# A two-layer graph network on one core: one-hots of the first column chunk by gather, remainders of five x tiles on GpSimd, one transpose moved

## The reference, cut to what matters

```python
agg = segment_sum(x[src], dst, num_segments=1250)
h   = (1 + eps) * x + agg
h   = relu(batch_norm(h @ W1 + b1, g1, be1))      # 512 -> 1024
h   = relu(batch_norm(h @ W2 + b2, g2, be2))      # 1024 -> 512
x   = layernorm(x + (x + h))
h   = relu(x @ V1 + c1) @ V2 + c2                 # 512 -> 256 -> 512
x   = layernorm(x + h + segment_sum(h[dst], src, num_segments=1250))
```

## Time and profile before

| | |
|---|---|
| median of 3 runs | 249.57 us (249.5 to 250.74) |
| the profiled execution | 249.95 us, of which the span takes 248.1 us |
| mean granted clock of TensorE | 0.995 of full speed |
| PE busy | 231.0 us, 93% of the span |
| DVE busy | 156.2 us, 63% |
| ACT busy | 134.2 us, 54% |
| POOL busy | 88.0 us, 35% |
| chain that ended last, by engine | PE 70%, DVE 12%, DMA 7%, ACT 6% |

### The profile page before, as it was taken

How to read it: one execution, slowest core, us unless ns; L and a number is a source line. 1 busy time by engine, 2 the same in 40 slices (tenths; PEclk the granted TensorE clock), 3 DMA queues, 4 the chain that set the end, 5 groups by cost and what they waited for, 6 DMA issues and landing times.

```text
span 248.1 us, 3897 instructions
## 1 busy us (share of the span) xinstructions
PE 231.0 (93%) x1454; PEld 197.3 (80%) x1454; DVE 156.2 (63%) x362; ACT 134.2 (54%) x233; POOL 88.0 (35%) x83
## 2 busy tenths in 40 slices
PE   0858999999999999999999999999999999999990
PEld 0845997777888888888888888888889997888970
DVE  1669899873966344555544316264876899796374
ACT  0656774763868067444455504457471639936373
POOL 5420000004920006565554500423456459701251
PEclk9999999999999999999999999999999999999998
DMA  3467800000066501111000087503209920000334
GB/s 100 156 214 214 202 0 3 1 3 3 3 261 239 198 1 45 42 42 45 0 0 0 4 206 142 106 3 60 45 4 170 202 85 3 0 0 0 131 127 160
DMA packets 32323, 19.96 MB, mean 80 GB/s; under 512 B 21927, under 2 KB 27084, under 8 KB 32302
## 3 DMA queue, kind: packets, MB, share of 16 engines
q1 hardware_dynamic: 31796, 19.45, 28.6%
q0 software_dynamic: 160, 0.13, 0.2%
q10 hardware_dynamic: 346, 0.10, 0.2%
HBM read 8.51 MB, written 5.92 MB: 58 GB/s over the span
## 4 chain that ended last, share of the span: by engine, by line
PE 70%; DVE 12%; DMA 7%; ACT 6%; issue 2%; POOL 1%; SPq 1%; DVEq 0%
PE ps L1281 22%; PE ps L1220 17%; PE ps L1298 11%; PE ps L1344 9%; PE ps L1362 6%; PE ps L1311 3%; DVE hot_s L849 3%; DMA plane_T<-planes 2%; PE ps L1200 2%; DMA src_i<-in_src 2%; DVE xT L984 2%; DMA pairs<-pair 2%; ACT planes L715 1%; DVE small_t L942 1%; DMA run<-pairs,start_i 1%
## 5 line engine op out<-in xcount | busy, mean ns | idle before, releaser
L942 DVE BATCH_NORM_STATS2 small_t<-ps 128x6 f32<-128x500 f32 (+1 forms) x36 | 21.6, 599 | 38.7 <-PE ps L1281 25.2
L1220 PE MATMUL ps<-AT,xh 128*128 128x500 f32 (+2 forms) x120 | 42.6, 366 | 0.4 <-ACT AT L569 0.4
L1220 PE MATMUL ps<-AT,xl 128*128 128x500 f32 (+2 forms) x120 | 40.9, 352 | 0.0
L1281 PE MATMUL ps<-h0h,wh 128*128 128x500 f32 (+1 forms) x96 | 33.9, 353 | 0.0
L1281 PE MATMUL ps<-h0h,wl 128*128 128x500 f32 (+1 forms) x96 | 33.9, 353 | 0.0
L1281 PE MATMUL ps<-h0l,wh 128*128 128x500 f32 (+1 forms) x96 | 33.8, 352 | 0.0
L485 POOL TENSOR_TENSOR wl<-w2s,wh 128x512 fp32r<-128x512 f32 x8 | 11.1, 1384 | 43.9 <-ACT wh L689 43.9
L480 POOL TENSOR_TENSOR wl<-w1s,wh 128x512 fp32r<-128x512 f32 x8 | 10.1, 1301 | 45.7 <-ACT AT L569 45.7
L1220 PEld LDWEIGHTS ps<-AT,xh 128*128 128x128 f32 (+1 forms) x120 | 22.6, 188 | 3.3 <-ACT AT L569 0.6
L1220 PEld LDWEIGHTS ps<-AT,xl 128*128 128x128 f32 (+1 forms) x120 | 22.7, 189 | 2.7
L1298 PE MATMUL ps<-a1h,wh 128*128 128x500 f32 (+1 forms) x96 | 23.7, 355 | 0.0
(11 more groups left out here) (148 smaller groups left out, 508.2 us busy)
## 6 DMA issues: line engine op xcount, KB each, us to landing
turns<-half_out SPq DMA_DIRECT2D x10, 320.0 KB, 2.2
out<-x SPq DMA_DIRECT2D x9, 256.0 KB
w1s<-in_L_gnn_W SPq DMA_DIRECT2D x4, 512.0 KB, 7.1
w2s<-in_L_gnn_W SPq DMA_DIRECT2D x8, 256.0 KB, 2.7
xs<-in_x SPq DMA_DIRECT2D x1, 1280.0 KB, 7.9
xs<-in_x SPq DMA_DIRECT2D x1, 1024.0 KB
lws<-in_L_gnn_W SPq DMA_DIRECT2D x1, 512.0 KB, 4.0
lw2s<-in_L_gnn_W SPq DMA_DIRECT2D x1, 512.0 KB, 4.2
```

Source lines behind the costliest of these rows:

```text
L942: link(nc.vector.bn_stats(stats[:, 6 * c:6 * c + 6], ps[:, zbank(t, c), 0:c1 - c0]))
L1220: last = mm(o, part[0:r, k, d * P:d * P + P], AT[0:r, k, c0:c1], start=(k == 0 and j == 0), stop=(k == NT - 1 and j == 1))
L1281: last = mm(ps[:, zbank(t, c), 0:c1 - c0], w[:, t, d * P:d * P + P], h[c][:, d, :], start=(d == 0 and j == 0), stop=(d == DT - 1 and j == 2))
```

## The change

**Keys.** The tiles `keyT` and `loT` keep their size, but their first 50 columns are used in another order: first the 25 windows of chunk 0 for c = 0, then the same windows for c = 1 (`keyW`, `loW`). `early_keys(c)` splits these 25 columns of one gather; `late_keys(c)` splits the other 100 windows later, behind the one-hots of group 4. The 50 columns make up groups 0 to 4 in this order, so groups 0 and 1 need the first gather alone, group 2 needs both, groups 3 and 4 the second. ACT copies them out with another pattern, in two pieces for group 2 (`early_out`). PSUM banks 6 and 7 hold the transposed runs until `late_keys` has read them; fill-in matmuls go to bank 4. The DVE queue waits for `keys_read` before it reads the flag.

**Remainders.** `xl` of tiles 5 to 9 is made by POOL, each when its `xh` is there, and `low_at` is gone.

**Transposes.** x's tile 5 is transposed once behind `build(3)`, tile 6 behind `build(5)` in the fast branch (PE has by then added tile 0's sums), where it was transposed behind `build(4)` before. Tiles 7 and 8 go one and two groups later.

```diff
         def x_bank(k):
-            return 3 + k if k < half else 6 + k % 2
+            return 3 + k if k < half else 5 if k == half else 6 + k % 2
+
+        key_bank, fill_bank = (6, 7), 4
...
-        cols_at = {6: half + 2, 7: half + 3, 11: half + 4}
-        turn_at = {6: half + 2, 7: half + 3, 12: half + 4}
+        cols_at = {5: half + 1, 7: half + 2, 9: half + 3, 11: half + 4}
+        turn_at = {5: half + 1, 7: half + 2, 9: half + 3, 12: half + 4}
         high_at = {5: half, 8: half + 1, 9: half + 2, 10: half + 3, 11: half + 4}
-        low_at = {7: half, 10: half + 1, 11: half + 2, 12: half + 3, 13: half + 4}
-        early_cols = {EARLY - 3: half, EARLY - 1: half + 1}
+        early_cols = {EARLY - 2: half}
...
+            for j, k in enumerate(range(half, NT)):
+                pl.wait_ge(xh_set, k + 1)
+                nc.gpsimd.tensor_tensor(xl[0:rows[k], k, :], xs[0:rows[k], k, :],
+                                        xh[0:rows[k], k, :].bitcast(F32), ALU.subtract).then_inc(xl_pool, 1)
+
             pl.wait_ge(AT_set, NG)
...
+            def early_keys(c):
                 v.wait_ge(rel_T, c + 1)
...
+                f = slice(c * WE, (c + 1) * WE)
+                link(split(keyW[:, f], loW[:, f], ps[:, key_bank[c], 0:WE]))
+
+            def late_keys(c):
+                split(keyT[:, WE:NW, c], loT[:, WE:NW, c], ps[:, key_bank[c], WE:NW]).then_inc(keys_read, 1)
...
+            shifted(0)
+            early_keys(0)
+            early_hots(0)
+            shifted(1)
+            early_hots(1)
+            early_keys(1)
+            early_hots(2)
+            early_hots(3)
+            v.wait_ge(counted, 1)
+            nc.vector.tensor_scalar(flag[0:1, :], ps[0:1, 2, 0:1], float(-2 * E), None,
+                                    ALU.not_equal).then_inc(flag_set, 1)
+            early_hots(4)
+            late_keys(0)
+            late_keys(1)
+            v.wait_ge(keys_read, 2)
             v.wait_ge(flag_set, 1)
             bad = v.value_load(flag[0:1, 0:1], min_val=0, max_val=1)
             with v.If(bad == 0):
                 for g in range(EARLY, NG):
                     one_hots(g)
-                    if g in low_at:
-                        x_low(low_at[g])
...
-            for g in range(EARLY):
-                build(g)
-                if g == 0:
-                    count()
-                if g in early_cols:
-                    x_cols(early_cols[g])
-                elif g < EARLY - 1:
-                    between((2, 4, 4, 4)[g])
+            keys(0)
+            pe.wait_ge(xT_set, fill_bank - 2)
+            between(8)
+            build(0)
+            keys(1)
+            between(3)
+            build(1)
+            count()
+            between(4)
+            build(2)
+            between(4)
+            build(3)
+            x_cols(early_cols[3])
+            build(4)
```

More of the change, by code:

```diff
@@ L186, in gnn_kernel @@
         loT = misc("loT", [P, NW, 2], BF16)
+        WE = CH[0][1] // WIN
+        keyW, loW = (t[:, 0:WE, :].rearrange("p w c -> p (w c)") for t in (keyT, loT))
         win_col, win_pair, ones, bounds = small(2), small(2), small(1), small(2)
@@ L565, in x_high, with early_out @@
                 nc.scalar.activation(xh[0:rows[k], k, :], xs[0:rows[k], k, :], ACT.Copy).then_inc(xh_set, 1)
+            def early_out(g):
+                act.wait_ge(built, g + 1)
+                for c, w0, w1, j in early_runs(g):
+                    last = nc.scalar.activation(
+                        AT[:, :, 0:CH[0][1]].rearrange("p k (w c d) -> p k w c d", c=2, d=SUB)[:, :, w0:w1, c, :],
+                        ps[:, g % 2, j * KEYS:(j + w1 - w0) * KEYS].rearrange("p (w d k) -> p k w d", d=SUB, k=NT),
+                        ACT.Copy)
+                last.then_inc(AT_set, 1)
             def group_out(g):
@@ L583, in w1_high @@
                     act.wait_ge(w1_in, 16 * DT)
-                    act.wait_ge(xl_set, NT)
+                    act.wait_ge(xl_set, half)
+                    act.wait_ge(xl_pool, NT - half)
                     act.wait_ge(x_turned, NT)
@@ L605, in _ @@
             for g in range(EARLY):
-                group_out(g)
+                early_out(g)
                 if g in early_cols:
@@ L832, in _, with shifted @@
                 x_low(k)
-            v.wait_ge(const, 4)
-            for c in range(2):
+            def shifted(c):
                 s = slice(c * RUN, (c + 1) * RUN)
@@ L839, in _, with split, early_hots @@
                                         ALU.subtract, ALU.subtract).then_inc(rel_set, 1)
-                v.wait_ge(rel_T, c + 1)
-                link(nc.vector.tensor_scalar(keyT[:, :, c], ps[:, c, 0:NW], LIFT, LIFT, ALU.add, ALU.subtract))
-                link(nc.vector.scalar_tensor_tensor(out=loT[:, :, c], in0=ps[:, c, 0:NW], scalar=P / 2 - 0.5,
-                                                    in1=keyT[:, :, c], op0=ALU.add, op1=ALU.subtract))
+            def split(key, lo, turned_rel):
+                link(nc.vector.tensor_scalar(key, turned_rel, LIFT, LIFT, ALU.add, ALU.subtract))
+                return nc.vector.scalar_tensor_tensor(out=lo, in0=turned_rel, scalar=P / 2 - 0.5, in1=key,
+                                                      op0=ALU.add, op1=ALU.subtract)
+            def early_keys(c):
+                v.wait_ge(rel_T, c + 1)
+                f = slice(c * WE, (c + 1) * WE)
+                link(split(keyW[:, f], loW[:, f], ps[:, key_bank[c], 0:WE]))
+            def late_keys(c):
+                split(keyT[:, WE:NW, c], loT[:, WE:NW, c], ps[:, key_bank[c], WE:NW]).then_inc(keys_read, 1)
+            def early_hots(g):
+                if g >= 2:
+                    v.wait_ge(built, g - 1)
+                f = slice(g * 2 * WG, (g + 1) * 2 * WG)
+                lo, key = (t[:, f].rearrange("p (w i) -> p w i", i=2)[:, :, None, :] for t in (loW, keyW))
+                nc.vector.tensor_tensor(
+                    hot_s[g % 2][:, :, :, :], iota2[:, None, :, :].broadcast_to([P, WG, P, 2]),
+                    lo.broadcast_to([P, WG, P, 2]), ALU.is_equal).then_inc(hot, 1)
+                nc.vector.tensor_tensor(
+                    hot_k[g % 2][:, :, :, :], iota_k[:, None, :, :].broadcast_to([P, WG, KEYS, 2]),
+                    key.broadcast_to([P, WG, KEYS, 2]), ALU.is_equal).then_inc(hot, 1)
             def one_hots(g):
@@ L1160, in x_cols @@
                     pe.wait_ge(xT_set, max(half, k - 1))
+                if k > half:
+                    pe.wait_ge(keys_read, min(k - half, 2))
                 for d in range(DT):
@@ L1175, in between, with keys @@
                 for _ in range(n):
-                    mm(ps[:, x_bank(0), 0:2 * P], flat[:, 0:P], flat, start=True, stop=True)
-            pe.wait_ge(const, 6)
[L1179 to L1183, removed]
+                    mm(ps[:, fill_bank, 0:2 * P], flat[:, 0:P], flat, start=True, stop=True)
+            def keys(c):
+                pe.wait_ge(xT_set, key_bank[c] - 2)
+                pe.wait_ge(rel_set, c + 1)
+                nc.tensor.transpose(ps[:, key_bank[c], 0:NW], rel[0:NW, c * RUN:(c + 1) * RUN],
+                                    ident[0:NW, 0:NW]).then_inc(rel_T, 1)
+            pe.wait_ge(const, 6)
             def count():
@@ L1214, in aggregate @@
                     else:
-                        pe.wait_ge(xT_set, half)
+                        pe.wait_ge(xT_set, half + 1)
                 if i == 0:
-                    pe.wait_ge(xl_set, k + 1)
+                    pe.wait_ge(*((xl_set, k + 1) if k < half else (xl_pool, k - half + 1)))
                 r = rows[k]
```

16 lines of the change are left out of this document (7 added, 9 removed).

## The result

| | before | after |
|---|---|---|
| median | 249.72 us (6 runs) | 253.28 us (6 runs, 253.09 to 253.96) |
| ratio | 1 | 1.0134, 95% interval 1.0119 to 1.0150 |
| profiled execution, span | 249.95, 248.1 us | 253.12, 251.3 us |
| mean granted clock | 0.995 | 0.990 |

The change makes the kernel slower, by 3.3 us by the ratio and 3.6 by the medians. I had said slower, by 1.9 us, and a range up to 252.9 us, which doesn't hold the measured 253.28.

What follows compares the result with a forecast made beforehand. DVE and PE were taken as close to level in groups 5 to 14, with DVE deciding after the change: +0.56 (late splits, flag), -0.92 (pauses filled), +2.25 (stops) give 1.9 us later, 251.5 us; range 249.8 to 252.9.

Steps and rivals of the forecast that it cites:

- the rival: Rival in the experiments, not the prediction: the remainders on POOL are the whole loss; no chance given.
- Step 1: First chunk by gather: first one-hot 1.87 us earlier, first sum 1.16 earlier, counting only through Step 2.
- Step 2: Late splits (1.22 us) and open flag load (0.5) ahead of group 5's one-hots: these start 0.56 us later.
- Step 3: Tile 6's transpose between builds of groups 5 and 6: 0.44 us of PE, hidden under DVE.
- Step 4: Remainders on POOL, groups 5 to 14: each of five stops DVE 1.05 us instead of taking 0.60, +2.25 us.
- without a pause: DVE from group 5 to group 14 takes 14.88 us with no pauses, since PE's builds are always ahead.
- The end of the stretch: Group 14's one-hots start at 38.15 instead of 36.26; its build and all behind come 1.9 us later.
- The corners of load and stop: Load from 0 to 1.0 us and a stop from 0.9 to 1.3 span +0.7 to +3.6 us.
- B: Rival: POOL doesn't hinder DVE's one-hots, PE sets the pace, -0.43 us, 249.1 us; chance 0.15.
- C: Rival: POOL runs in DVE's pauses or shares, a stop costs 0.6 to 0.9, +0.4, 250.0 us; chance 0.10.
- D: Rival: one-hots keep POOL out, late remainders `xl` of tiles 7 and 8 hold up PE, +3.4, 253.0 us; chance 0.05.

Runs made afterwards that it cites:

- 5: Changed kernel with remainders back on DVE, flag loaded ahead of the late splits, six fill-in matmuls ahead of the first sum: 251.1 us, ratio 1.0041.
- 10: Changed kernel with flag loaded ahead of the late splits, six fills ahead of the first sum and fifteen ahead of group 13's build: 251.64 us, ratio 1.0047.
- 4: Changed kernel with six fill-in matmuls ahead of the first sum and six ahead of group 5's build: 253.2 us, ratio 1.0122.
- 3: Changed kernel with the flag loaded ahead of the four late splits instead of behind them: 253.22 us, ratio 1.0109.
- 2: Kernel before with only the remainders of tiles 5 to 9 moved to POOL: 252.7 us, ratio 1.0099.
- 1: Changed kernel with the remainders of tiles 5 to 9 back on DVE, in their places of before: 250.79 us, ratio 1.0028.
- 9: As 5, but tiles 7 and 8 transposed behind groups 6 and 7 as in the kernel before: ratio 0.9990.
- 11: Kernel before with the flag loaded only when group 4's one-hots are done: 250.88 us, ratio 1.0016.
- 7: Kernel before with four extra subtractions on POOL, which read SBUF, beside DVE's one-hots: 255.58 us, ratio 1.0215.
- 8: As 7, but POOL only writes, three memsets at each of the four places: 251.21 us, ratio 1.0036.

## Why the prediction was right in its direction and wrong in its size

The loss can be laid out by the start of the products, from 78.92 before. Without the stops, load hidden, fills in (5): 78.79. With POOL's remainders and the late fills (10): 80.79, **2.0 us for the stops**. With the load laid open (4): 81.50, **0.7 for the load**. Without fills (the changed kernel): 82.08, **0.6 for the clock** in the profiled execution, and 1.4 where it falls between 39.5 and 43 (3 against 10: 82.18 against 80.79, and 0.6% of the time). These are differences of single profiled executions of four kernels. The medians carry the clock's part in 10 and 3. For the stops they give 2.5 us (2), 2.7 (changed kernel against 1) and 1.4 (10 against 9), but only 0.15 for 10 against 5, since 5 loses 1.4 us behind the products; so 2.0 is one value within 1.4 to 2.7. By the medians the remainders on POOL are 1.0 to 1.1% of the 1.3%: the rival was wrong, but not by much.

- *Step 1, the chunk by gather:* right. Forecast 15.42 for the first `hot_s`, 21.20 for group 4's `hot_k`, 22.94 for the first sum; measured 15.38, 21.08 and 22.70. By itself it was worth nothing that 9 could show, as said.
- *Step 2, late splits and load:* mis-sized. For load and branch I took 0.5, the middle between nothing and 1.0 us; it is 1.02 in the changed kernel and 1.03 in 11, the upper bound. The splits took 1.05 from 21.41 to 22.46, not 1.22. So group 5's `hot_s` came at 23.48 instead of 23.27.
- *Step 3, tile 6's transpose:* at full clock it lay under DVE's delay as forecast (in 4 PE waited 0.15 for `hot_k` behind it). At half clock it took 1.09 and put `build(6)` at 26.00, 0.3 behind the end of its `hot_k`. And I looked only at PE's side of the moved transposes. On ACT, tile 8's copy moved ahead of `xh` of tile 7, and so held it back (0.86 us at 33.11 in the changed kernel). What that cost with the remainders on POOL no run shows; POOL's last three remainders followed each other without a gap, but so did three in 2, where the transposes stand as before.
- *Step 4, the stops:* the mechanism is shown by 2, 7 and 8, and the size of one was right, 1.06 to 1.10 for 1.05. But four of the five came in full; the first fell mostly into a pause of DVE and cost 0.18. Together they took 4.51 us, not 5.25, and this luck hid 0.74 of what follows.
- *"without a pause (PE's builds, which free the buffers, are always ahead of DVE)":* **this step failed.** With the clock at half from 24.4 to 27.9 PE fell behind, and DVE waited 0.82 and 0.39 us for builds. From group 5's to group 14's `hot_s` it took 15.73 us, not 14.88: 9.63 for the pairs, 4.51 for the stops, and 1.59 for pauses that I had put at nothing. Kernel 4, with the clock kept up, took 15.03, of which stops were 5.00 and pauses 0.40. So at full clock too the step was wrong by 0.40, and the half clock cost another 0.70 net.
- *The end of the stretch:* all stops came ahead of group 13's build, not 14's, and PE had then still a tile's sums to do, so that group 14's build came 0.21 later than DVE alone would have it.

From 1.9 us forecast this gives 1.9 + 0.21 (step 2) + 0.85 (15.73 for 14.88) + 0.21 (the end) = 3.17, against 3.16 measured at the products. The forecast had **no term for the clock** at all. The corners of load and stop, +0.7 to +3.6, would have held the 3.16; the range that I gave, up to 252.9, cut them. Rivals B and C are excluded by the stretched rows, though in 3, 4 and 10 the first remainder waited for a pause of DVE, as C has it. D's wait of PE for `xl` didn't occur. B's sum, -0.43 us, would have needed PE at full clock as well.

## What to carry to other kernels

Before work moves to GpSimd, look in the trace for a row in which VectorE, with two inputs in SBUF, ran beside a GpSimd instruction that reads SBUF. If it's stretched, the move can cost VectorE most of the GpSimd instruction's duration (here 1.08 of 1.27 us) instead of its own 0.60. Give the clock a term of its own where a change opens pauses on TensorE, look at the windows' granted clock behind each, and compare the mean clocks of executions of one kernel: a lower one went with 0.3 us in the kernel before and with 1.2 in kernel 1. A load of a flag into a register belongs ahead of the waits that it doesn't need (0.7 us at the products, 4 against 10). And a moved step must be followed on every engine's queue that it's moved within, ScalarE's too.

## What the runs showed of the hardware that I had not expected

GpSimd doesn't always get its turn at the first end of a VectorE row. In kernel 10 POOL's first remainder was asked for at 26.23, took 3.20 us instead of 1.27, and got in only behind four one-hot rows, in DVE's next pause, as in kernels 3 and 4; the following ones got in behind one or two rows:

```profile
26.23 3.20 POOL L489 TENSOR_TENSOR xl<-xs,xh 128x512 fp32r<-128x512 f32 x1 [12.44 <-ACT xh L580]
30.04 1.56 POOL L489 TENSOR_TENSOR xl<-xs,xh 128x512 fp32r<-128x512 f32 x1 [0.60 <-ACT xh L580]
```

Pauses of TensorE of only 0.7 to 1.8 us were followed by 3.5 us at half clock (7 in kernel 11) in some executions and not in others: the profiled executions of kernel 4 and of the changed kernel had a 1.77 us pause ahead of group 13's build and kept their clock, kernel 3's had such a pause and lost it. What decides between the two was not tried. The load of one flag and the branch behind it took 1.02 and 1.03 us on VectorE where nothing hid them, and GpSimd's memsets, which read nothing, stretched no one-hot at all.
